# Moving the maxima products, one value unit and the dense step inside the attention windows of a two-layer decoder kernel

## The reference

```python
x = x + jnp.tanh(g_xattn[0]) * _L0_xattn_ref(_layernorm(x), ctx, ctx, mask, ...)   # linear attention
x = x + jnp.tanh(g_ffn[0]) * _L0_ffn_ref(_layernorm(x), w_gate, w_up, w_down)      # quantised feed-forward
x = x + jnp.tanh(g_xattn[1]) * _L1_xattn_ref(_layernorm(x), ctx, ctx, mask, ...)   # softmax attention
x = x + jnp.tanh(g_ffn[1]) * _L1_ffn_ref(_layernorm(x), gate_w, w1, b1, w2, b2)    # mixture of experts
# _L1_xattn_ref, 16 heads of width 8:
scores = jnp.einsum('bhqd,bhkd->bhqk', qh, kh) / jnp.sqrt(jnp.float32(D_K))
attn = jax.nn.softmax(scores, axis=-1)
context = jnp.einsum('bhqk,bhkd->bhqd', attn, vh)
# _L0_ffn_ref: rows and weights are rounded to small integers before each product:
scale = 127.0 / jnp.clip(jnp.max(jnp.abs(x), axis=-1, keepdims=True), 1e-05)
xq = jnp.clip(jnp.round(x * scale), -128.0, 127.0) / scale
```

## Time and profile before

| | us |
|---|---|
| median of 3 runs | 771.31 (769.78 to 772.39) |
| the profiled execution | 770.22 |
| its span | 768.4 |
| one steady pair of windows (318.77 to 372.67) | 53.90 |
| all windows (237.51 to about 651) | 414 |

### The profile page before, as it was taken

How to read it: one execution, slowest core, us unless ns; L and a number is a source line. 1 busy time by engine, 2 the same in 40 slices (tenths; PEclk the granted TensorE clock), 3 DMA queues, 4 the chain that set the end, 5 groups by cost and what they waited for, 6 DMA issues and landing times.

```text
span 768.4 us, 19268 instructions
## 1 busy us (share of the span) xinstructions
PE 671.1 (87%) x7283; PEld 469.5 (61%) x7283; DVE 538.7 (70%) x1252; ACT 510.4 (66%) x807; POOL 270.7 (35%) x324
## 2 busy tenths in 40 slices
PE   3599999997367899899999999999999988899997
PEld 3477777775124566566556666665666566467777
DVE  5799999998967887788778877878877761312122
ACT  4487777775425787787787777787788777443431
POOL 4398888883341132324314313313332110000000
PEclk9899999999668999999999999999999999799999
DMA  4122222253460763475376356537644671211110
GB/s 141 40 81 81 80 80 80 80 156 58 62 139 13 158 143 92 109 171 108 77 159 131 94 118 137 125 88 165 133 99 112 131 153 36 62 31 41 44 41 25
DMA packets 59379, 74.42 MB, mean 97 GB/s; under 512 B 35320, under 2 KB 40178, under 8 KB 59306
## 3 DMA queue, kind: packets, MB, share of 16 engines
q1 hardware_dynamic: 59306, 73.39, 40.4%
HBM read 32.35 MB, written 1.40 MB: 44 GB/s over the span
## 4 chain that ended last, share of the span: by engine, by line
PE 49%; DVE 9%; issue 7%; ACT 3%; POOL 2%; SPq 1%; DMA 1%; DVEq 0%; POOLq 0%; ACTq 0%
PE ps L741 9%; PE ps L654 8%; PE ps L814 7%; PE ps L802 7%; PE ps L728 6%; PE ps L646 4%; DVE mx L1584 4%; PE ps L640 4%; ACT P L992 1%; PE ps L676 1%; POOL KP L1101 1%; DVE silu L1499 1%; DMA QS<-QD 1%; SPq L442 1%; DVE QS L1590 1%
## 5 line engine op out<-in xcount | busy, mean ns | idle before, releaser
L992 ACT ACTIVATE P<-ps,kbias,kscale 125x896 f32<-125x896 f32 x192 | 210.3, 1098 | 92.8 <-PE ps L728 89.2
L1584 DVE TENSOR_REDUCE mx<-ps 128x1 f32<-128x500 f32 x336 | 215.6, 671 | 51.7 <-PE ps L654 49.0
L654 PE MATMUL ps<-KP,Qb 128*128 128x500 bf16 x336 | 129.0, 386 | 15.8 <-DVE mx L1584 7.1
L1101 POOL TENSOR_TENSOR KP<-kvall,KP 128x1500 bf16<-128x1500 f32 x16 | 48.6, 3040 | 226.1 <-ACT KP L935 226.1
L741 PE MATMUL ps<-P,Vp 125*32 125x112 f32 x3072 | 114.2, 266 | 1.4 <-ACT P L992 1.2
L741 PEld LDWEIGHTS ps<-P,Vp 125*32 125x32 f32 x3072 | 67.6, 109 | 48.7 <-issue 32.2
L531 PE MATMUL ps<-wkv,cT 128*125 128x256 f32 x384 | 91.9, 383 | 0.8 <-ACT arena L892 0.8
L531 PEld LDWEIGHTS ps<-wkv,cT 128*125 128x125 f32 x384 | 69.3, 190 | 9.9 <-issue 1.1
L728 PE MATMUL ps<-QS,KS 128*128 128x112 bf16 x768 | 70.1, 215 | 5.8 <-issue 4.3
L728 PE MATMUL ps<-QS,arena 128*128 128x112 bf16 x768 | 68.2, 215 | 6.9 <-issue 4.3
L728 PEld LDWEIGHTS ps<-QS,KS 128*128 128x128 bf16 x768 | 55.9, 99 | 28.9 <-issue 8.6
(11 more groups left out here) (213 smaller groups left out, 1017.4 us busy)
## 6 DMA issues: line engine op xcount, KB each, us to landing
cT<-ctxT_dram SPq DMA_DIRECT2D x32, 750.0 KB, 4.2
KS<-KP SPq DMA_DIRECT2D x48, 375.0 KB, 7.3
arena<-KP SPq DMA_DIRECT2D x48, 375.0 KB, 7.2
QS<-QD SPq DMA_DIRECT2D x96, 28.0 KB, 5.7
wgu<-w_dram SPq DMA_DIRECT2D x8, 256.0 KB, 3.1
silu<-w_dram SPq DMA_DIRECT2D x8, 256.0 KB, 3.0
x<-xh_dram SPq DMA_DIRECT2D x1, 512.0 KB, 3.6
mixed<-att SPq DMA_DIRECT2D x16, 28.0 KB
```

Source lines behind the costliest of these rows:

```text
L654: ins = nc.tensor.matmul(ps[:, bank, 0:KCW], q[:, 128 * c:128 * c + 128], KP[par][0][:, KCW * k:KCW * k + KCW], start=True, stop=True)
L992: nc.scalar.activation(P[t % 2][0:TK, :].rearrange("p (k n) -> p k n", k=2), src, ACT.Exp, scale=kscale[0:TK, bass.ds(n, 1)], bias=kbias[0 ...
L1101: nc.gpsimd.tensor_tensor(KP[par][2][:], krest, KP[par][1][:], ALU.subtract).then_inc(sem("kp3_ready"), 1)
L1584: ins = v.tensor_reduce(mx[:, c, k:k + 1], ps[:, bank, 0:KCW], AX.X, ALU.max)
```

## The change

The table is written anew, and the points that depend on it follow.

```diff
 PLACES = [
     [[["MX0"], ["Q1"], ["MX1"]], [["MX2"], [], ["AT", "MX3"]], [["MX4"], ["OT"], ["MX5"]],
-     [["MX6"], ["V0"], ["MX7"]], [["MX8"], ["DE"], ["MX9"]], [["MX10"], ["K0"], ["MX11"]],
-     [["MX12"], ["V1"], ["MX13"]], [["MX14"], ["K1"], ["MX15"]], [["MX16"], ["FT"], ["MX17"]],
-     [["MX18"], ["K2"], ["XT", "MX19"]], [["MX20"], ["V2"], ["G"]], [["SH"], [], []]],
+     [["MX6"], ["DE"], ["MX7"]], [["MX8"], ["V0"], ["MX9"]], [["MX10"], ["K0"], ["MX11"]],
+     [["MX12"], ["V1", "MX13"], ["MX14"]], [["MX15"], ["K1"], ["MX16"]], [["MX17"], [], ["XT", "MX18"]],
+     [["MX19"], ["K2"], ["MX20"]], [[], ["FT"], ["G"]], [["SH"], ["V2"], []]],
     [[["MX0"], ["FO"], ["MX1"]], [["MX2"], ["V0"], ["U", "MX3"]], [["MX4"], ["OT"], ["MX5"]],
-     [["MX6"], ["V1"], ["MX7"]], [["MX8"], ["K0"], ["MX9"]], [["MX10"], ["HT"], ["MX11"]],
-     [["MX12"], ["V2"], ["DN", "MX13"]], [["MX14"], ["K1"], ["MX15"]], [["MX16"], ["ET"], ["MX17"]],
-     [["MX18"], ["K2"], ["MX19"]], [["MX20"], ["LT"], []], [["SH"], [], []]],
+     [["MX6"], ["V1", "MX7"], ["MX8"]], [["MX9"], ["K0"], ["MX10"]], [["MX11"], ["HT"], ["MX12"]],
+     [["MX13"], [], ["DN", "MX14"]], [["MX15"], ["K1"], ["MX16"]], [["MX17"], ["ET"], ["MX18"]],
+     [["MX19"], ["K2"], ["MX20"]], [[], ["LT"], []], [["SH"], ["V2"], []]],
 ]
...
                         exponentials(w, par, t, fixed(i) and w == 0)
+                        if t == 0 and "Q1" in has:
+                            chain(at, "Q1", i + 1)
                         if t == 0 and "OT" in has:
                             take_sums(at, w - 1)
...
-                        elif unit == "MX11":
+                        elif unit == "MX9":
                             first_sum(n)
-                        elif unit == "MX13":
+                        elif unit == "MX12":
                             quantise(n)
-                        elif unit == "MX16":
+                        elif unit == "MX15":
                             quantised(n)
```

More of the change, by code:

```diff
@@ L1023, in pair1 @@
                             elif unit in CHAIN:
-                                if unit not in ("DE", "U", "DN"):
-                                    chain(at, unit, i + (1 if unit == "Q1" else 2))
+                                if unit not in ("DE", "U", "DN", "Q1"):
+                                    chain(at, unit, i + 2)
                             elif unit == "FT":
```

## The result

| | us |
|---|---|
| before, median of 4 runs | 770.78 (769.78 to 772.39) |
| changed, median of 4 runs | 760.22 (759.28 to 760.72) |
| ratio | 0.9859, 95% interval 0.9841 to 0.9876 |
| profiled execution of the changed kernel | 760.72, span 758.9 |

The change made the kernel 10.6 us faster (1.4%). The forecast was 762.6, with a range of 757.5 to 769.5.

The account below looks back on a forecast made before the run. PE was taken to bound the kernel, so only its waits could be gained: 770.22 less 12.6 gained plus 3.9 of costs gives 761.5 us profiled, 762.6 as median with 1.1 added; range 757.5 to 769.5.

Parts of the forecast that it names:

- What bounds the kernel: PE, busy 87% of the span; windows last as long as its instructions and waits, so only waits can go.
- the sum: Profiled 770.22 us less 12.6 gained plus 3.9 of costs gives 761.5; the median, 1.1 higher, should be 762.6.
- V2 behind SH: Window ends: the value unit, 1.10 us long, covers PE's wait for the QS copies; all 14 waits go, 8.6 us.
- `gate`: After even windows: V2's delay of PE covers most of the first maximum's wait for `gate`; 2.0 us gained.
- MX20 up: Odd windows: this maximum comes half a tile or more earlier, ending SH's waits for `mneg`; 1.4 us gained.
- Window 0: There `quantise` falls later into POOL's Qb and loses about 0.6 us less; 0.6 us gained.
- Bank 6: Window ends: V2, then FO and Q1, wait for ACT to free this bank; costs 1.2 and 0.6 us.
- the slower rival: Window ends: V2's or FT's copy misses its gap on ACT, PE waits a whole exponential; 775 us, chance 0.06.
- The packed tiles and DN without V2: Odd windows: three maxima in a tile and V2's leaving make MX14 wait; cost 2.1 us, bounds 0 and 4.2.
- The rule weighed: POOL and DVE share ports, so K0's rest waits 0.3 us inside Qb in five windows; up to 1.5 us slower.
- XT and the maxima of even windows: Even windows: waits of 3.7 us for maxima and 2.4 for XT change places, with no difference it could call.
- What was to cost nothing: SP's later context load, ACT's Q1 ahead of the sums, and window 14, staying at 23.3 us: no loss.

## Why the prediction was right

**What bounds the kernel** was read rightly: all of the gain is PE's waits. The profiled execution took 760.72 us where the sum gave 761.5, and windows 3 and 4, the pair of 53.90, took 52.31 where the text gave 52.6. The median came out at 760.22, 2.4 under the forecast: 0.8 of this is the sum's, 1.1 was added because the median of before lay that much above its profiled execution, and the changed kernel's median lies 0.5 below its own. In the windows alone the sum gave 8.7 and the traces 10.4.

**V2 behind SH**, 8.6 us: the wait of the first scores went from 8.6 to nothing, and V2 alone gave 9.9. Confirmed by doing it alone and by undoing it alone. The sum missed that V2 had a wait of its own where it stood in odd windows: it started 0.46 us behind the scores instead of 0.20 (386.94 to 387.40), and the 0.1 of it that the profile names is for ACT's copy of HT, ahead of it in bank 6. In window 5 its leaving took 1.24 us from that tile (from the scores to `weigh`, 1.53 became 0.29), and at the window's end, from the scores behind SH to the next window's, 1.56 became 1.86 with V2 in between. That is 0.94 gained, not 0.61, and some 1.6 us more over the six odd windows.

**`gate`**, 2.0 us: too high. In windows 5, 7 and 9 the first maxima product now comes 0.48 us after its scores (368.66 to 369.14), in windows 1, 3 and 11 0.38, where it was 0.68 and is 0.21 in the other kind of window. That is 0.2 and 0.3 gained, 1.5 in all. V2 covers one microsecond, the wait for QS takes 0.6 to 0.7 of it, and the copies started 0.52 after SH in that window (366.60 to 367.12) where the prediction counted 0.43.

**MX20 up**, 1.4: right. SH starts 0.31 behind its scores (340.18 to 340.49), and no wait for `mneg` is left in windows 0 to 13.

**Window 0**, 0.6: `quantise` lost 0.55 less there (0.99 for 1.54), as worked out, but PE's wait fell from 1.59 to 0.60:

```profile
252.25 0.99 DVE L1468 TENSOR_SCALAR xn<-x,mv,rstd 128x128 f32<-128x128 f32 x1
```

is DVE's row of the changed kernel, and PE's is

```profile
254.58 0.38 PE L654 MATMUL ps<-KP,Qb 128*128 128x500 bf16 x1 [0.60 <-DVE mx L1586]
```

The term was 0.4 too small. What DVE loses and what PE waits are not the same number; the prediction had the first and needed the second.

**Bank 6**, 1.8 us of cost for V2, FO and Q1: did not appear. No row of V2, FO or Q1 waits for ACT. The rows had said so for V2, since LT's copy ends 0.2 before V2 is due; the prediction took a price nevertheless. With it falls the slower rival.

**The packed tiles and DN without V2**, 2.1 us: too small, and the largest error of the sum. The wait at MX14 is there, 0.49 in each odd window, where the prediction had 0.7 less a wait of 0.35 before:

```profile
385.02 0.39 PE L654 MATMUL ps<-KP,Qb 128*128 128x500 bf16 x1 [0.49 <-DVE mx L1586]
```

That 0.35 is in no row. Before, the product behind DN followed it at 0.23 (388.99 to 389.23 in window 5), and the next one came 0.2 late. From DN to its maxima product it is now 0.89, which is 0.66 more, less the 0.2: 0.46 net. The packed tile adds 0.3 to each odd window, about 0.78 together and 4.7 us in six windows, 2.6 more than the sum had. The two parts stood under one name in it, and the experiments part them: the wait at MX14 comes from V2's leaving, the late products of tile 3 from the packing. Moving K0's rest behind DN took 0.45 of the 0.49 away. No run unpacks tile 3 and leaves the rest.

**The rule weighed**, the ports shared by POOL and DVE: K0's rest ran 1.26 us, 0.58 longer, instead of the 0.3 that the prediction gave it. By the version with K0's rest later, it cost the even windows 0.31 to 0.45 each, 1.8 in five, with what its place in the queue may have to do with it. The prediction put it beside the sum, at up to 1.5 us. What the Trainium skill, SBUF — State Buffer, "Who interferes with whom", says, that the instruction which comes second waits for the whole of the other, is what four kernels here show: 1.26, 1.75 and 0.96 us on DVE, each ending 0.1 to 0.5 us behind Qb's end, and 0.66 where Qb was over.

**XT and the maxima of even windows** stood in the sum with nothing, as a change that could not be called. Even windows 2 to 10 are together 1.1 us shorter in the changed kernel than with V2 alone moved, in spite of the 1.8 that K0's rest costs.

**What was to cost nothing** did: the Q1 order (26.11 in both), SP's later load, and window 14, which lasted 23.13 us for 23.28 and still ended with a wait of 2.35 for the stacking DMAs.

So the mechanism was right, and the closeness of the number is in part luck. Against the 8.7 us of the sum, `gate` gave 0.5 less and MX14 with the packed tile cost 2.6 more; bank 6 cost 1.8 less, V2 gave 1.6 more in odd windows, the even windows 1.1 more and window 0 0.4 more. Together this makes 10.5, where the windows measured 10.4. These are distances between starts in single windows, times the windows, and good to some tenths. Errors as large as 2.6 us cancelled, and left the profiled execution 0.8 and the median 2.4 below the forecast.

## What to carry to other kernels

When PE is nearly always busy, look for the few places where it hands a result to another engine and has to have it back at once, and put a piece of independent work there that is long enough to cover the way back: that one move was worth 9.9 of 10.6 us. Then read what the piece covered where it stood before, since that wait opens up again (0.49 us here). A list of waits with a least length hides what is shorter: here 0.34 us a window in two pieces, found by the distances between starts and by comparing windows of two kernels. And when work moves on an engine that shares ports with another, look up what the other runs at that minute: the same delay of one small step gained 0.31 us per window in one order of the program and lost 0.66 in another.

## What the runs showed that I had not expected

- K0's rest, a step on DVE with two inputs in SBUF, ends about 0.5 us behind the end of POOL's Qb when it starts inside it: K0's rest at 357.97 took 1.26 and at 360.33 took 1.75 us, against 0.66 to 0.68 when alone. Which of two DVE instructions falls into Qb makes little difference to DVE, but much to PE: with quantise inside, an even window lasted 1.22 us longer than in the version that keeps both out of Qb (27.02 and 25.80), with K0's rest inside 0.31 longer (26.11); in the version with V2 and K0's rest alone moved, where K0's rest met Qb's start, it was 0.66 longer than with V2 alone moved.
- The version with only K0's rest moved further, a change of one number, beats both kernels: 755.99 us, 0.981 of before (0.9794 to 0.9827).
